# Results of a stage taken in one slot later, and key scores that start behind eleven row tiles instead of fourteen

## What is computed

```python
x = x + 0.5 * _L0_ffn_ref(_layernorm(x), ...)                      # a: mixed low-rank experts
x = x + _L0_attn_ref(_layernorm(x), ...)                           # w: attention in windows
x = x + 0.5 * _L0_ffn_ref(_layernorm(x), ...)                      # b: the experts again
x = x + 0.5 * _L1_ffn_ref(_layernorm(x), weight, bias)             # c: product on a 6-bit grid
x = x + _L1_attn_ref(_layernorm(x), W_DQ, ...)                     # m: low-rank attention, 8 heads
x = x + 0.5 * _L1_ffn_ref(_layernorm(x), weight, bias)             # d: as c

def _L1_ffn_ref(x, weight, bias):                                  # c and d
    xq, xs = _mx_quantize(x2)      # per 32 values: scale by the largest, round to the grid
    wq, ws = _mx_quantize(w2)
    return (xq * xs) @ (wq * ws).T + bias

def _L1_attn_ref(...):                                             # m
    c_q = h_t @ W_DQ + b_DQ
    c_kv = h_t @ W_DKV + b_DKV
    ...
    scores = jnp.einsum('bhsd,bhtd->bhst', q, k) * scale
    attn = softmax(scores)
    o = jnp.einsum('bhst,bhtd->bhsd', attn, v_c)
    return o @ W_O + b_O
```

## Time and profile before

| what | us |
|---|---|
| median of three runs | 1821.54 (1814.57 to 1821.82) |
| the execution that was profiled | 1816.68 |
| its span in the trace | 1814.9 |
| PE busy in the span | 1664.2 |
| slots of b and c, from the first `dve_mixed` to the first `query` | 94.4 |
| opening of m, from there to the first key score | 27.8 |
| one batch of m in its middle | 148.8 |

### The profile page before, as it was taken

The page is one execution under the profiler, slowest core; times in us unless marked ns, Lnnn a source line. Parts: engine busy times, 40 slices in busy tenths (PEclk is TensorE's granted clock), DMA queues, the critical chain, the costliest instruction groups (busy, mean ns, idle before and its releaser), DMA issues.

```text
span 1814.9 us, 39662 instructions
## 1 busy us (share of the span) xinstructions
PE 1664.2 (92%) x15057; PEld 1217.1 (67%) x15057; DVE 1388.4 (77%) x2976; ACT 1138.4 (63%) x2222; POOL 1178.1 (65%) x909
## 2 busy tenths in 40 slices
PE   4679899999877899999999999999999999999995
PEld 3557777777665567676766766766676677677674
DVE  5557677776577888878888888888887888888862
ACT  5447677777676456666656566666656756665662
POOL 4300100110165398898898988989889898898892
PEclk9889999999977899999999999999999999999997
DMA  4556666664000000000001001001001000100101
GB/s 123 139 138 156 161 148 165 153 156 106 29 1 1 1 8 9 11 7 9 8 9 20 7 11 19 11 7 19 10 9 21 7 10 7 21 8 10 19 10 30
DMA packets 198676, 81.47 MB, mean 45 GB/s; under 512 B 152552, under 2 KB 177492, under 8 KB 198356
## 3 DMA queue, kind: packets, MB, share of 16 engines
q1 hardware_dynamic: 198484, 78.93, 19.5%
HBM read 39.79 MB, written 29.88 MB: 38 GB/s over the span
## 4 chain that ended last, share of the span: by engine, by line
PE 53%; DVE 11%; POOL 2%; issue 1%; ACT 1%; DMA 0%; SPq 0%; POOLq 0%; ACTq 0%
PE pair L1824 12%; PE pair L1877 11%; PE pair L1881 11%; PE pair L1935 10%; DVE amax L1832 4%; PE pair L1928 4%; PE pair L1649 2%; DVE o_inv L1945 1%; PE pair L1640 1%; POOL w_mix L1906 1%; DVE stats L485 1%; PE pair L1663 1%; DVE q_low L1753 1%; DVE key_hl L1767 1%; DVE cq L1764 1%
## 5 line engine op out<-in xcount | busy, mean ns | idle before, releaser
L1892 ACT ACTIVATE prob<-pair 128x512 f32<-128x512 f32 x1024 | 604.7, 598 | 420.4 <-PE pair L1881 342.2
L1832 DVE TENSOR_REDUCE amax<-pair 128x1 f32<-128x512 f32 x1024 | 670.4, 682 | 133.9 <-PE pair L1824 131.8
L1824 PE MATMUL pair<-key_hl,q_hi 128*128 128x512 f32 x1024 | 437.4, 429 | 11.4 <-DVE amax L1832 8.1
L1877 PE MATMUL pair<-q_hi,key_hl 128*128 128x512 f32 x1024 | 404.5, 395 | 2.6 <-ACT prob L1892 2.6
L1881 PE MATMUL pair<-q_low,key_h 65*128 65x512 f32 x1024 | 405.3, 396 | 0.0
L1906 POOL TENSOR_TENSOR w_mix<-w_mix,prob 128x1024 f32<-128x1024 f32 x160 | 382.3, 2389 | 24.8 <-ACT prob L1892 8.2
L1906 POOL TENSOR_TENSOR Wm<-Wm,prob 128x1024 f32<-128x1024 f32 x155 | 369.8, 2386 | 20.8 <-ACT prob L1892 4.1
L520 POOL TENSOR_SCALAR veps<-mv 128x8 f32<-128x8 f32 x47 | 11.4, 243 | 460.5 <-DVE mv L493 459.7
L1824 PEld LDWEIGHTS pair<-key_hl,q_hi 128*128 128x128 f32 x1024 | 195.4, 191 | 117.2 <-issue 51.1
L1935 PE MATMUL pair<-prob,values 128*32 128x256 f32 x4096 | 246.0, 380 | 0.0
L1186 DVE TENSOR_REDUCE mx_neg<-pair 128x4 f32<-128x512 f32 x256 | 164.8, 686 | 94.5 <-PE pair L1090 93.8
(11 more groups left out here) (209 smaller groups left out, 2222.3 us busy)
## 6 DMA issues: line engine op xcount, KB each, us to landing
rows_mem<-once SPq DMA_DIRECT2D x128, 128.0 KB, 2.0
queries<-rows_mem SPq DMA_DIRECT2D x64, 256.0 KB, 4.6
keys<-rows_mem SPq DMA_DIRECT2D x16, 1024.0 KB, 7.3
rows_mem<-once SPq DMA_DIRECT2D x128, 64.0 KB, 1.9
q_low<-shift_cols SPq DMA_DIRECT2D x512, 0.5 KB, 2.0
yT<-o_norm SPq DMA_DIRECT2D x256, 32.0 KB, 1.9
x<-x_dram SPq DMA_DIRECT2D x8, 512.0 KB, 7.3
out_dram<-x SPq DMA_DIRECT2D x7, 512.0 KB, 3.4
```

The source lines that it names most:

```text
L1824: e.matmul(row_bank(("row", r, i)), q_hi[:, k, t * P:(t + 1) * P], key_hl[:, b % 2, i * HALF:(i + 1) * HALF], start=True, stop=True, skip_ ...
L1832: e.tensor_reduce(amax1[:, u % 2, t, i:i + 1], row_bank(("row", r, i)), AX_X, ALU.max).then_inc(*row_maxed.up((r, i)))
L1877: e.matmul(bank(j), key_hl[:, b % 2, ks], q_hi[:, k, sl], start=True, stop=False, skip_group_check=True)
L1892: e.activation(prob1[:, g % P_BUFS, half * HALF:(half + 1) * HALF], bank(K_BANKS[(2 * g + half) % 3]), ACT.Exp, scale=SCALE1).then_inc(*ke ...
```

## The change

There are four edits. First, DVE adds the result of stage c one slot later: `dve_c_result(i - 3)` stands behind the begin of the norm, where `dve_c_result(i - 2)` stood at the end of the slot. On POOL the fills and the two extra norms go one slot later, behind the dequantisation. Second, the first `query` moves ahead of the last product of slot 8, in bank 3. Third, `const` and `value` no longer follow each other in one step, and the last batch's turn and product come later. Fourth, `key_step` maps step g to the key tile n: g + 3 up to g = 3, g + 2 up to 11, g + 1 up to 19, then g; steps 4, 12 and 20 have no key tile. Row tiles and small products keep their steps.

The edit of `dve_low_part` is needed for the opening, where both `cq` come before both `key_hl`, but it stands in the function that all batches use: `key_hl` is now part 4, in the step after `cq`.

```diff
@@ -224,6 +224,13 @@
...
 PIPELINE = 16
+KEY_PAUSES = 4, 12, 20
+def key_step(g):
+    return None if g in KEY_PAUSES else g + sum(g < pause for pause in KEY_PAUSES)
 Q_BUFS, P_BUFS = 3, 8
@@ -248,15 +255,18 @@
...
+    def prepare_first():
+        return [*prepare(0)[0:4], ("query", 0, 0), *prepare(0)[4:6]]
...
             u, rest = divmod(g + 16 - 4 * i, NT)
-            if rest == 0 and 0 <= u < U:
+            if rest == 0 and 0 <= u < U and u + i:
                 return "query", u, i
...
     opening = {"bias": [((("bias", 0, 0), None, None), 1)]}
-    for item, j in zip(prepare(0), (2, 3, 4, 5, 2, 3)):
+    for item, j in zip(prepare_first(), (2, 3, 4, 5, 3, 2, 3)):
         run = begin(item, j)
...
@@ -1372,6 +1382,9 @@
...
                         pe_low_part(e, item, j, before, part)
+                else:
+                    for (item, j, before), part in opening_m["query"]:
+                        pe_low_part(e, item, j, before, part)
                 if i < 2:
...
@@ -1400,6 +1413,9 @@
...
                     act_c_turned(e, i - 2)
+                if i == B:
+                    for (item, j, before), part in opening_m["query"]:
+                        act_low_part(e, item, j, before, part)
                 if i + 2 < B:
...
@@ -1411,26 +1427,28 @@
...
                     norm_begin_dve(e, "c", i)
+                if i == 2:
+                    dve_low_weights(e, 2)
+                if i >= 3:
+                    dve_c_result(e, i - 3)
+                if i == B:
+                    for (item, j, before), part in sorted(opening_m["low"], key=lambda run: run[1]):
+                        dve_low_part(e, item, j, before, part)
                 if i >= 1:
                     norm_scale(e, "c", i - 1, NT // 2, NT)
-                if i == B:
-                    for (item, j, before), part in opening_m["low"]:
-                        dve_low_part(e, item, j, before, part)
-                if i >= 1:
                     dve_c_scale(e, i - 1)
...
                     dve_low_weights(e, 1)
-                elif i == 2:
-                    dve_low_weights(e, 2)
                 elif i == 3:
...
                     norm_begin_dve(e, "m", 0)
-                if i >= 2:
-                    dve_c_result(e, i - 2)
+            for (item, j, before), part in opening_m["query"]:
+                dve_low_part(e, item, j, before, part)
+            dve_c_result(e, B - 2)
...
@@ -1439,6 +1457,19 @@
...
                     pool_dequantise(e, "w", c_q8[:, 1, 0:NQ, :], scale_w[:, :], wd, NQ)
+                if i == 3:
+                    e.wait_ge(*dequant.at(("c", i - 2)))
+                    e.memset(key_h1[KR:KR + 1, :, :].bitcast(F32), 1.0).then_inc(*set_low.up("key row"))
+                    e.wait_ge(*set_low.at("key row"))
+                elif i == 4:
+                    norm_pool(e, "b", B - 1, True)
+                elif i == 5:
+                    e.wait_ge(*dequant.at(("c", i - 2)))
+                    e.memset(cq[QR:QR + 2, :, :].bitcast(F32), 1.0).then_inc(*set_low.up("query rows"))
+                    e.wait_ge(*set_low.at("query rows"))
+                    e.memset(ones_col[:, :], 1.0).then_inc(*set_low.up("ones"))
+                elif i == 6:
+                    norm_pool(e, "m", 0, True)
                 if i < B:
...
@@ -1446,24 +1477,11 @@
...
                     pool_c_scale(e, i - 1)
-                if i == 3:
-                    norm_pool(e, "b", B - 1, True)
-                elif i == 5:
-                    norm_pool(e, "m", 0, True)
-                elif i == 2:
-                    e.wait_ge(*scaled.at(("c", i - 1)))
-                    e.memset(key_h1[KR:KR + 1, :, :].bitcast(F32), 1.0).then_inc(*set_low.up("key row"))
-                    e.wait_ge(*set_low.at("key row"))
-                elif i == 4:
-                    e.wait_ge(*scaled.at(("c", i - 1)))
-                    e.memset(cq[QR:QR + 2, :, :].bitcast(F32), 1.0).then_inc(*set_low.up("query rows"))
-                    e.wait_ge(*set_low.at("query rows"))
-                    e.memset(ones_col[:, :], 1.0).then_inc(*set_low.up("ones"))
             pool_c_dequantise(e, B - 1)
...
-        CONST_AT, LAST_C = -13, {"turn": -12, "copy": -10, "product": -9, "result": -7}
+        FIRST, LAST_C = {-12: "const", -11: "value"}, {"turn": -10, "copy": -9, "product": -8, "result": -6}
@@ -1764,6 +1782,7 @@
...
                     *cq_ready.up((a, i)))
+            elif kind == "low" and part == 4:
                 e.scalar_tensor_tensor(out=key_hl[KR:P, k, sl], in0=bank(j)[0:KR, :], scalar=b_low[0:KR],
...
@@ -1801,8 +1820,9 @@
...
                 row_uses += [("row", g + ROW_LEAD, i) for i in range(2)]
-            if g % NT == 3 and 0 <= g // NT - 1 < B * NH:
-                row_uses.append(("total", g // NT - 1, 0))
+            n = key_step(g)
+            if n is not None and n % NT == 3 and 0 <= n // NT - 1 < B * NH:
+                row_uses.append(("total", n // NT - 1, 0))
         row_place = {use: i for i, use in enumerate(row_uses)}
...
@@ -1991,36 +2011,37 @@
...
             for g, early, late in plan_m:
-                if g == CONST_AT:
-                    for kind in ("const", "value"):
-                        for (item, j, before), part in opening_m[kind]:
-                            pe_low_part(e, item, j, before, part)
+                n = key_step(g)
+                if g in FIRST:
+                    for (item, j, before), part in opening_m[FIRST[g]]:
+                        pe_low_part(e, item, j, before, part)
                 elif g == LAST_C["turn"]:
...
                     pe_c_product(e, B - 1)
-                elif g == 0:
+                elif n == 0:
                     e.wait_ge(*x_dve.at(("c", B - 1)))
...
                         pe_row_scores(e, g + ROW_LEAD, half)
-                    if 0 <= g < total:
-                        pe_key_scores(e, g, half)
+                    if n is not None and 0 <= n < total:
+                        pe_key_scores(e, n, half)
                 for (item, j, before), part in late:
                     pe_low_part(e, item, j, before, part)
-                if g % 4 == 3 and 0 <= g // 4 - 1 < total // 4:
-                    pe_weigh(e, g // 4 - 1)
+                if n is not None and n % 4 == 3 and 0 <= n // 4 - 1 < total // 4:
+                    pe_weigh(e, n // 4 - 1)
...
             for g, early, late in plan_m:
+                n = key_step(g)
                 if g == LAST_C["copy"]:
                     act_c_turned(e, B - 1)
-                elif g == 0:
+                elif n == 0:
                     e.wait_ge(*products.at(("c", B - 1, 1)))
...
                     act_low_part(e, item, j, before, part)
-                if 0 <= g < total:
-                    act_exponentials(e, g)
+                if n is not None and 0 <= n < total:
+                    act_exponentials(e, n)
...
@@ -2054,15 +2075,15 @@
...
             for g, early, late in plan_m:
-                if g == CONST_AT + 1:
-                    for kind in ("const", "value"):
-                        for (item, j, before), part in opening_m[kind]:
-                            dve_low_part(e, item, j, before, part)
+                n = key_step(g)
+                if g - 1 in FIRST:
+                    for (item, j, before), part in opening_m[FIRST[g - 1]]:
+                        dve_low_part(e, item, j, before, part)
                 elif g == LAST_C["result"]:
...
                     dve_low_part(e, item, j, before, part)
-                u, t = divmod(g - 11, NT)
+                u, t = divmod(n - 11, NT) if n is not None else (0, None)
                 if t == 1 and 0 <= u < B * NH:
...
@@ -2080,8 +2101,9 @@
...
                     pool_shift(e, *divmod((r - 4) // 4, 2))
-                if (g - 1) % NT in range(1, 7) and 0 <= g - 1 < total - NT:
-                    pool_sum(e, g - 1)
+                n = key_step(g)
+                if n is not None and (n - 1) % NT in range(1, 7) and 0 <= n - 1 < total - NT:
+                    pool_sum(e, n - 1)
         def pe(e):
...
```

## The result

The change makes the kernel slower: 1838.0 us as the median of four runs (1833.0 to 1841.2) against 1821.7 us, a ratio of 1.0102 with a 95% interval of 1.0077 to 1.0127. The profiled execution took 1838.9 us. Forecast were 1822.5 us and no change; the time lies outside the range of 1808 to 1833. The four runs of before lay high: in the sessions of the experiments its medians are 1816.9 to 1817.9 us, so the change costs about 20 us rather than 16.

What follows compares the result with a forecast made beforehand. PE was taken to bound the kernel, busy for 1664.2 of 1814.9 us. A gain of 10.4 us at step 21 against 13.9 us lost in m gave +3.5 us, so 1822.5 us, range 1808 to 1833.

Steps and rivals of the forecast that it cites:

- The slots and the opening: Before m: shorter slots, an earlier first query and fewer row tiles ahead of key scores gain 10.4 us at step 21.
- POOL's closed chain: In the slots: rounding, hand-overs, dequantisation, norm and scaling sum to about 7.8 us a slot; batch 6's scaling ends 8.1 us earlier.
- The collisions of the normalisation with POOL: In the slots: DVE's L513 meeting POOL's dequantisation takes up to 1.2 us longer a slot, hidden while DVE is ahead.
- The later part 4: In m: key_hl behind DVE's row maxima delays two queries a batch, losing 2.0 us a batch, 13.9 us in all.
- the small waits that the sum had counted: In m, first half of low: DVE loses 0.85 us and PE makes up 0.6 from its own small waits.
- the rival of absorption: In m: DVE catches up and PE's later waits shrink, so only 4 us are lost; 1809 to 1812, chance 0.27.
- The clock: In m: rival that longer stops lower the clock to 0.79 over 12 us, 17 us more, 1840; chance 0.08.
- one stretch with 3.1 us of idle: From 613.7 to 660.5 us in the kernel before: evidence that the clock stays at 1.00 despite idle PE.
- the row at 577.78: A turn in the slots of the kernel before: behind 2.17 us of waiting it took 1.91 us at the lower clock.
- The rival of the slots: In the slots: DVE or PE becomes last, gain at step 21 under 5 us; 1829 to 1833, chance 0.15.

Runs made afterwards that it cites:

- e5: The changed kernel with key_hl a step late only for the first half of low (and in the opening), right behind cq for the second; 1821.4 us.
- e6: The changed kernel with key_hl a step late only for the second half of low (and in the opening); 1819.5 us.
- e8: e1 without the mapping of steps to key tiles: key scores start behind fourteen row tiles again, without pauses; 1810.4 us.
- e9: e1 with key_hl of batches 1 to 7 between the two row maxima of the step of cq; 1815.8 us.
- e1: The changed kernel with key_hl of batches 1 to 7 back in part 3, right behind cq; in the opening still part 4; 1806.0 us.
- e3: The changed kernel with five matmuls, products unread, ahead of each of the 14 queries that wait for key_hl; 1821.2 us.
- e2: The kernel before with one edit alone, key_hl in part 4 for every batch; 1847.1 us.

## Why the prediction was wrong

**The slots and the opening: the mechanism right, the size in part by luck.** POOL's closed chain was the right thing to sum. The scaling of batch 6 was forecast 8.1 us earlier and is 7.1 earlier in the table. From its end to the first row scores I had 12.3 us at the clock of 0.50, and it took 10.5, since the turn and the query ran at 1.00 in this execution (1.10 and 0.48 us); in e5, e6, e8 and e9, with the same order, it took 12.1 to 12.9. So the first row scores came 9.6 us earlier instead of 8.4. From there to the first key scores 3.5 us were saved instead of 4.4, and until step 21 e1 gave back 3.7 instead of 2.4. These errors cancel: 13.1 us at the first key scores against 12.8 forecast, and in e1, which has no late `key_hl` in m, 9.4 at step 21 against 10.4. Hardly anything of it is due to the earlier key tiles (e8). The collisions of the normalisation with POOL came as the row had warned: its slowest single instruction takes 1.95 us now. They stayed off the path, since POOL was last.

**The later part 4, as stops: right.** I forecast 2.0 us a batch and 13.9 us in all. e3 shows 150.8 us a batch, as the first full batch of e2 does, and 12.6 us from step 21 to the last 32 key tiles; the first stop, which lies ahead of step 21, adds 1.6 us (149.5 less 147.9). Neither DVE nor PE made up more than the small waits that the sum had counted, so the rival of absorption fell.

**The clock: the step that failed.** I held it unlikely that stops of 1.6 to 2 us bring the clock down, because PE is nearly always busy on both sides, and gave this rival 0.08 and left it out of the range. This reason failed. The evidence was one stretch with 3.1 us of idle in all, in which the clock stayed at 1.00, and the row at 577.78, behind a wait of 2.17 us, that ran at the lower clock. I read the first as proof and used the second only in the slots. In its place the runs showed this: the stops came out at 1.75 us (2.72 the first) and 1.1 to 1.5 us, 11 to 13 us apart, and the clock fell in every one of the seven batches. It cost 16.4 us. I had priced the rival at 17, but by another picture, 0.79 over 12 us in every batch; what the trace shows is 0.50 for shorter or longer stretches, so the price was near by luck. The account: -7.8 us at step 21, the first stop included, and behind it +12.6 for the stops, +16.2 for the clock in the batches and +1.7 for the clock in the last unit are +22.7 at the last key score, as measured (1299.0 less 1276.3). The forecast had +3.5. The trace of before could not have settled this: the one wait of such a length that it has in m before the last key score, 1.79 us in the last unit, has the clock at 1.00 behind it, and the row at 577.78 the clock at 0.50. That was a reason to give the rival more than 0.08 and to keep it in the range, since no row showed what a second stop would do.

**The rival of the slots** fell: they shortened as forecast.

## What to carry to other kernels

An edit made for one place in a function that all places call is an edit everywhere: look for the waits that hang on the counter it moves, and read in the trace how much room they have. Where PE starts 0.06 us behind what it waits for, most of what goes ahead of that is lost: here a query that came 1.55 and one that came 1.2 us later (forecast) cost 2.0 us a batch. And where an engine that is nearly always busy gets a new stop, price the clock behind it as well as the stop, above all if a second stop follows soon.

## What the runs showed of the hardware

The granted clock of TensorE fell from 1.00 to 0.50 in each batch of the kernel after, where PE stood still for 1.75 us (2.72 in the first batch) and 11 to 13 us later for 1.1 to 1.5 us, and worked in between. It stayed there for up to 10.2 us although PE had no gap. In e2, with the same two stops, it fell in six batches of seven. With one of 1.75 us a batch, in e5, it fell in seven batches of seven; with one of up to 1.6 us, in e6, in one of seven; with two of 1.2 and 0.9 us, in e9, in none of six, and not behind the 2.13 us of e9's first batch either. The same late `key_hl` with matmuls in the stop (e3) left it at 1.00 in all seven batches. One and the same stop, of 1.7 to 1.8 us in the last unit, was followed by 0.50 in nine traces and by 1.00 in three. So the clock can fall behind a stop of this length and need not, and the length alone does not decide; what else does no run shows. In the batches of e3 what PE did in the stop decided, not how late the query came.

The Trainium skill, page TensorE: Matmul & The Clock Gate, Part 1, says that activity opens the gate and idleness closes it. e3 agrees with that; how little idleness was enough, 1.75 us in the batches of e5, is what I had not expected.
